# Ten extra products on TensorE between attention and the first tile of experts, and the early batches' sums moved ahead of b1's transpose

## The chip, the cores and the metric

The kernel runs on one core of a Trainium2 chip. The metric is the device time of one execution in microseconds (us). Engines: PE (TensorE), DVE (VectorE), ACT (ScalarE), POOL (GpSimd) and SP (SyncE, which here only issues DMAs).

## The reference

A gated cross-attention layer and a gated mixture of experts, over 8 batches of 112 tokens with 256 features:

```
x = x + tanh(g_xattn) * xattn(ctx, layernorm(x))      # 8 heads of 64, 375 context rows a batch, rotary keys
h = layernorm(x)
P = softmax(h @ Wg); top 2 of 8 experts, gates P_norm = P_topk / (sum P_topk + 1e-9)
y = sum over e of P_norm[e] * (gelu(h @ W1[e] + b1[e]) @ W2[e] + b2[e])   # W1: 256x1024, W2: 1024x256
x = x + tanh(g_ffn) * y
```

## The kernel before

The program has two blocks. `attention` works batch after batch and, beside its last heads, normalizes the rows for the experts and routes the first six batches (EARLY): top two experts, gates, and the slot in DRAM at which each token's row is kept for each of its two experts. The last two batches (LATE) finish attention only at the block's end.

`experts` is the second block, and the change lies in its PE part. Each engine has its own queue and goes through it in order; semaphores tie them together. What it does before the first tile:

- SP loads b1 as rows (`b1rows`, semaphore `small_loaded`), then b2 in eight copies (`b2x`), then expert 2's weights, then the rows of tiles 0 and 1 (`load_rows`, after all 16 scatters have landed), then stores `x_all` (after `b2_added` 4) and loads expert 3's weights.
- PE transposes b1rows into the bank `pm[0]` (L1545). Into the bank `pm[1]` it forms `sums`: the base (L1548), one product for each of the six early batches (L1551), and after `hits_done` 2 the late batches' (L1554) and the slots (L1556), which raises `slot_done`. It then transposes the gates `pnorm` (L1560, after `gated` and `b1t_done`), multiplies them by b2 in four products (L1568, after `pT_done`), and transposes the rows of tile 0 (`turn_rows`, L1578).
- DVE picks the late batches' two experts, forms their gates (to L143), waits for `slot_done`, makes the slots (`place`, L147 to L151), copies b1's transpose (`b1t`), works out the plan of the extra tiles (L1458 to L1476), the low half of W2 (L1479) and pT (L1482), and adds each b2 product to x_all (L1486). The third and fourth b2 product reuse a bank and wait for the first and second addition.
- POOL scatters the late batches' rows to their slots, two scatters a batch (L155), once the slots are there.
- ACT splits tile 0's transposed rows into high and low parts (`th`), DVE makes `tl`, and with it the first up product can run.

Then come 14 tiles of 256 rows. A tile has 48 up products (L1593 to L1595) and 48 down products (L1612 to L1614), in fp32r, three to each exact product; a bank `ph` takes up products, `py` down products. An f32 matmul of the program stands in the trace as two instructions. `ph[0]` is first written by the first up products.

Of the kernel before, what the change touches and what calls it, by code (L numbers as in the profile page):

```python
# [20 lines left out]
B, M, D = 8, 112, 256  # L21
# [3 lines left out]
E, FF = 8, 1024  # L25
# [10 lines left out]
FB = FF // P  # L36
# [1194 lines left out]
def experts(nc, w1, b1, w2, b2, out, rows_dram, acc_dram, x_all, rows1, rows2, router, ident, gates, w1s, w2s, w1n, w2n, wide, deep,  # L1231
            logit, w1_loaded, w2_loaded, w1h_done, w1l_done, w2h_done, w2l_done, filled):

    with ExitStack() as st:  # L1234
        def sb(name, shape, dt=F32):
            return st.enter_context(nc.sbuf_tensor(name, shape, dt))

        def ps(name):
            return st.enter_context(nc.psum_tensor(name, [P, 512], F32))

        def sem(name):
            return st.enter_context(nc.semaphore(name))
# [11 lines left out]
        b1rows = sb("b1rows", [E * FB, P])  # L1254
# [16 lines left out]
        ph = [ps(f"ph{n}") for n in range(3)]  # L1271
        pm = [ps("pm0"), ps("pm1")]

        small_loaded, b2_loaded = sem("esmall_loaded"), sem("b2_loaded")
        ptables_set, b2x_set, plan_done = sem("ptables_set"), sem("b2x_set"), sem("plan_done")
        ptr_done, pT_done, btr_done, b1t_done = (sem(n) for n in ("eptr_done", "pT_done", "btr_done", "b1t_done"))
# [264 lines left out]

        @block.tensor
        def _(pe):
            pe.wait_ge(small_loaded, 16)
            pe.transpose(pm[0][:, 0:E * FB], b1rows[:], ident[0:E * FB, 0:E * FB]).then_inc(btr_done, 1)  # L1545
            sums = pm[1][0:M, 0:3 * E].rearrange("q (b e) -> q b e", e=E)
            hit = router.hit
            pe.matmul(sums, router.ones[:], router.base[:].rearrange("q (a e) -> q a e", a=1).broadcast_to([M, 3, E]),  # L1548
                      start=True, stop=False)
            for b in range(B - 2):  # L1550
                pe.matmul(sums, router.ones[:], hit[:, b:b + 1].broadcast_to([M, 3, E]), start=False, stop=False)  # L1551
            pe.wait_ge(router.hits_done, 2)
            for b in range(B - 2, B):
                pe.matmul(sums[:, b - B + 3:3], router.ones[:], hit[:, b:b + 1].broadcast_to([M, B - b, E]),  # L1554
                          start=False, stop=False)
            pe.matmul(sums[:, 0:2], router.lower[:], hit[:, LATE], start=False, stop=True) \  # L1556
                .then_inc(router.slot_done, 1)
            pe.wait_ge(router.gated, 4)
            pe.wait_ge(b1t_done, 1)
            pe.transpose(pm[0][0:E * B, 0:M], router.pnorm[:].rearrange("q b e -> q (b e)"), ident[0:M, 0:M]) \  # L1560
                .then_inc(ptr_done, 1)
            pe.wait_ge(pT_done, 1)
            pe.wait_ge(b2_loaded, 16 * B)
            pe.wait_ge(plan_done, 2)
            for n in range(B // 2):
                if n >= 2:
                    pe.wait_ge(b2_added, n - 1)
                pe.matmul(pm[n % 2][0:M, :], pT[:], b2x[:, 2 * n:2 * n + 2].rearrange("q b d -> q (b d)"),  # L1568
                          start=True, stop=True).then_inc(b2_done, 1)

            def turn_rows(i):
                pe.wait_ge(xt_loaded[i % 3], 16 * (i // 3 + 1))
                if i:
                    pe.wait_ge(tl_done, i)
                for k in range(KD):
                    for n in range(2):
                        c = k * T + n * P
                        last = pe.transpose(pxt[:, c:c + P], xt[i % 3][:, n, k * P:(k + 1) * P], ident[:])  # L1578
                last.then_inc(tr_done, 1)

            def up(i, g):
                n = i * GRP + g
                if g == 0:
                    pe.wait_ge(w1l_done, KD * (i + 1))
                    pe.wait_ge(tl_done, i + 1)
                if n >= 3:
                    pe.wait_ge(gelu_done, n - 2)
                p = i % 2
                for u in range(2):
                    dst = ph[n % 3][:, u * T:(u + 1) * T]  # L1590
                    c = slice((2 * g + u) * P, (2 * g + u + 1) * P)
                    for k in range(KD):
                        pe.matmul(dst, w1h[p][:, k, c], th[:, p, k], start=k == 0, stop=False)  # L1593
                        pe.matmul(dst, w1h[p][:, k, c], tl[:, p, k], start=False, stop=False)  # L1594
                        last = pe.matmul(dst, w1l[p][:, k, c], th[:, p, k], start=False, stop=k == KD - 1)  # L1595
                last.then_inc(up_done, 1)

            def down(i, g):
                n = i * GRP + g
                if g == 0 and i:  # L1600
                    pe.wait_ge(y0_done, i)
                    pe.wait_ge(y1_done, i)
                if g % 2 == 0:
                    pe.wait_ge(w2l_done, 2 * i + g // 2 + 1)
                pe.wait_ge(hl_done, n + 1)
                p = i % 2
                for u in range(2):
                    f = 2 * g + u
                    for s in range(2):
                        c = slice(s * P, (s + 1) * P)  # L1610
                        dst = py[s][:, 0:D]
                        pe.matmul(dst, hh[:, n % 3, u, c], w2h[p][:, f], start=f == 0, stop=False)  # L1612
                        pe.matmul(dst, hh[:, n % 3, u, c], w2l[p][:, f], start=False, stop=False)  # L1613
                        last = pe.matmul(dst, hl[:, n % 3, u, c], w2h[p][:, f], start=False, stop=f == FB - 1)  # L1614
                last.then_inc(down_done, 1)

            turn_rows(0)
            for i in range(TILES):
                up(i, 0)
                if i:  # L1620
                    down(i - 1, 2)
                up(i, 1)
                if i:
                    down(i - 1, 3)
                up(i, 2)
                if i + 1 < TILES:
                    turn_rows(i + 1)
                down(i, 0)
                up(i, 3)
                down(i, 1)  # L1630
            down(TILES - 1, 2)
            down(TILES - 1, 3)
# [32 lines left out]
```

## Time and profile before

| | |
|---|---|
| time, 3 runs | 526.6 us median, 524.97 to 527.88 |
| the profiled execution | 523.4 us, span 521.7 us, mean granted PE clock 0.928 |
| PE busy | 446.3 us, 86% of the span |
| PE weight loads busy | 373.2 us, 72% |
| DVE, ACT, POOL busy | 289.4, 295.1, 195.4 us |

The span is from the first to the last instruction of the profiled execution. The granted clock is TensorE's, as a share of 2.4 GHz: 1.00 is that, 0.50 is 1.2 GHz. "Idle before" is the time an engine stood idle ahead of an instruction, with what ended it.

### The profile page before, as it was taken

The page shows a single profiled execution, that of the slowest core. Times are in us where ns is not written, and L with a number is a line of the kernel's source. Part 1 is how long each engine was busy: PE and PEld are TensorE (multiplying, and loading weights), DVE is VectorE, ACT ScalarE, POOL GpSimd, SP SyncE. Part 2 cuts the span into 40 slices and gives each one's busy share as a digit, 9 for nine tenths or more (in the row PEclk, how much of TensorE's full clock was granted, in tenths as well). Part 3 has the DMA queues.
Part 4 walks back from the last instruction along what each step waited for, and adds up shares of the span by engine and source line. Part 5 has one row for each costly group of instructions (what it writes and reads, how often), then busy time and mean ns, then how long its engine had stood idle before and what let it go on. Part 6 is the DMA issues. An engine that isn't in the chain of part 4 may idle for free. (4 is left out here: it accounts for less than half of the span.)

```text
span 521.7 us, 9510 instructions
## 1 busy us (share of the span) xinstructions
PE 446.3 (86%) x3237; PEld 373.2 (72%) x3237; DVE 289.4 (55%) x707; ACT 295.1 (57%) x652; POOL 195.4 (37%) x223
## 2 busy tenths in 40 slices
PE   2674699999989999899998764589999999999990
PEld 1453476766767677676776643279999999999990
DVE  3784324244451634435254823558888888888850
ACT  3534466765666666766767411056667667776730
POOL 4530163462825538164460165302222222333222
PEclk9976699999999999999999875569999999999997
DMA  7400010000000008999000021785777778775323
GB/s 190 117 29 1 1 31 0 9 24 2 29 1 24 5 0 252 226 215 319 12 2 1 1 71 44 233 254 175 212 204 212 219 223 232 224 206 132 44 29 90
DMA packets 41864, 56.04 MB, mean 107 GB/s; under 512 B 1745, under 2 KB 37153, under 8 KB 41808
## 3 DMA queue, kind: packets, MB, share of 16 engines
q1 hardware_dynamic: 36864, 49.80, 32.2%
q0 software_dynamic: 4960, 5.72, 7.1%
q8 instruction: 23, 0.38, 0.3%
q14 instruction: 17, 0.14, 0.1%
HBM read 40.37 MB, written 16.07 MB: 108 GB/s over the span
## 5 line engine op out<-in xcount | busy, mean ns | idle before, releaser
L1367 POOL DMA_INDIRECT acc_scratch<-yv,xt x28 | 49.2, 1757 | 130.6 <-DVE yv L1520 126.3
L1389 ACT ACTIVATE hf<-ph,b1t 128x256 f32<-128x256 f32 x112 | 47.0, 471 | 48.4 <-PE ph L1595 47.8
L871 DVE TENSOR_REDUCE negmax<-sc 112x1 f32<-112x487 f32 x64 | 42.2, 660 | 46.4 <-PE sc L1103 46.4
L691 ACT ACTIVATE prob<-sc,negmax 112x487 f32<-112x487 f32 x64 | 43.5, 680 | 12.6 <-DVE negmax L871 9.4
L1128 PEld LDWEIGHTS po<-probt,vals 125*64 125x64 f32 (+1 forms) x512 | 25.4, 139 | 23.5 <-issue 15.6
L699 ACT COPY probt<-pt 125x448 f32<-125x448 f32 x64 | 34.7, 542 | 11.1 <-PE pt L1111 10.9
L1103 PE MATMUL sc<-keys,queries 64*112 64x488 f32 x128 | 35.3, 629 | 6.1 <-ACT keys L640 3.4
L1502 DVE TENSOR_TENSOR hl<-hf,hh 128x512 fp32r<-128x512 f32 x56 | 38.8, 693 | 1.9
L1111 PEld LDWEIGHTS pt<-ident,prob 112*125 112x125 f32 x256 | 36.6, 191 | 4.2
L1111 PE MATMUL pt<-ident,prob 112*125 112x112 f32 x256 | 38.3, 274 | 0.0
L1500 DVE CAST hh<-hf 128x512 fp32r<-128x512 f32 x56 | 24.2, 433 | 23.7 <-ACT hf L1389 23.2
L379 POOL TENSOR_TENSOR krot<-krow,rope_t 125x512 f32<-125x512 f32 x21 | 27.0, 1285 | 22.1 <-ACT krow L618 22.0
L492 POOL TENSOR_TENSOR cl<-cf,ch 128x250 fp32r<-128x250 f32 x24 | 17.5, 728 | 45.3 <-ACT ch L612 45.3
L1593 PE MATMUL ph<-th,wide_h 128*128 128x256 f32 x112 | 32.6, 291 | 1.5 <-DVE tl L1491 1.5
L1128 PE MATMUL po<-probt,vals 125*64 125x112 f32 (+1 forms) x512 | 32.5, 270 | 1.2 <-ACT probt L699 1.2
L880 DVE TENSOR_TENSOR heads<-out_t,po 128x112 f32<-128x112 f32 x32 | 8.7, 271 | 43.4 <-ACT out_t L707 43.4
L1594 PE MATMUL ph<-tl,wide_h 128*128 128x256 f32 x112 | 32.5, 290 | 0.0
L1595 PE MATMUL ph<-th,wide_l 128*128 128x256 f32 x112 | 32.3, 288 | 0.0
L1612 PE MATMUL py<-deep_h,hh 128*128 128x256 f32 x112 | 32.0, 285 | 0.0
L1612 PE MATMUL py<-w2h_odd,hh 128*128 128x256 f32 x112 | 31.9, 285 | 0.0
L1593 PE MATMUL ph<-th,w1h_odd 128*128 128x256 f32 x112 | 31.6, 282 | 0.0
L1594 PE MATMUL ph<-tl,w1h_odd 128*128 128x256 f32 x112 | 31.6, 282 | 0.0
(273 smaller groups left out, 1372.1 us busy)
## 6 DMA issues: line engine op xcount, KB each, us to landing
w_next<-in_L_ffn_W SPq DMA_DIRECT2D x10, 1024.0 KB
rows_scratch<-blank SPq DMA_DIRECT2D x2, 4257.0 KB, 33.4
w_third<-in_L_ffn_W SPq DMA_DIRECT2D x8, 1024.0 KB
w1s<-in_L_ffn_W SPq DMA_DIRECT2D x5, 1024.0 KB
w2s<-in_L_ffn_W SPq DMA_DIRECT2D x5, 1024.0 KB, 8.7
xt<-rows_scratch SPq DMA_DIRECT2D x14, 258.0 KB, 2.8
ctx_t<-in_ctx SPq DMA_DIRECT2D x8, 375.0 KB
w1s<-in_L_xattn_Wkv SPq DMA_DIRECT2D x1, 1024.0 KB, 12.3
```

The costliest lines, as they stand in the source:

```text
L691: act.activation(prob[:, h % 2, 0:JA], sc[h % 2][0:M, 0:JA], ACT.Exp, bias=negmax[:, h % 2:h % 2 + 1], accum_out=total[:, p, h:h + 1]).the ...
L699: act.copy(probt[:, h // 2 % 2, :, h % 2, :], pt[h % 2][0:JR, 0:NT * M].rearrange("q (a r) -> q a r", a=NT)) \
L871: dve.tensor_reduce(negmax[:, h % 2:h % 2 + 1], sc[h % 2][0:M, 0:JA], AX, ALU.max, negate=True).then_inc(max_done.sem, 1)
L1103: pe.matmul(sc[u][0:M, 0:JP], queries[r, p, a], keys[r, p, a], start=True, stop=True, tile_position=(u * DH, 0)).then_inc(score_done.sem, 1)
L1111: last = pe.transpose(pt[h % 2][0:JR, j * M:(j + 1) * M], prob[:, h % 2, j * JR:(j + 1) * JR], ident[0:M, 0:M])
L1128: pe.matmul(po[r, 0:M], vals[0:rows, p, j, a * P + u * DH:a * P + (u + 1) * DH], probt[0:rows, a % 2, j, u], start=j == 0, stop=j == NT - ...
L1367: pool.indirect_dma_start(out=acc_dram, out_offset=bass.IndirectOffsetOnAxis(ap=xt[i % 3][:, n, D + 1:D + 2].bitcast(I32), axis=0), in_=yv ...
L1389: last = act.activation(hf[:, n % 3, u], ph[n % 3][:, u * T:(u + 1) * T], ACT.Gelu, bias=b1t[:, col])
L1502: dve.tensor_tensor(hl[:, n % 3], hf[:, n % 3], hh[:, n % 3].bitcast(F32), ALU.subtract) \
L1593: pe.matmul(dst, w1h[p][:, k, c], th[:, p, k], start=k == 0, stop=False)
L1594: pe.matmul(dst, w1h[p][:, k, c], tl[:, p, k], start=False, stop=False)
L1612: pe.matmul(dst, hh[:, n % 3, u, c], w2h[p][:, f], start=f == 0, stop=False)
```

## The change

PE gets a helper `idle(n)` that issues n products nobody reads: the identity's first 112 rows (112 x 128) as weights, 512 columns of `rows1` as data, f32, into `ph[0]`. It is called with 2 at five places: at the block's start, after b1's transpose, after the slots' product, after the transpose of the gates, and ahead of `turn_rows(0)`. The base product and the six early batches' products now stand ahead of the wait for b1's rows and of b1's transpose.

```
-            pe.wait_ge(small_loaded, 16)
-            pe.transpose(pm[0][:, 0:E * FB], b1rows[:], ident[0:E * FB, 0:E * FB]).then_inc(btr_done, 1)
+            def idle(n):
+
+                for _ in range(n):
+                    pe.matmul(ph[0][:], ident[0:M, :], rows1[:, 0:2, 0:D], start=True, stop=True)
+
+            idle(2)
             sums = pm[1][0:M, 0:3 * E].rearrange("q (b e) -> q b e", e=E)
             hit = router.hit
             pe.matmul(sums, router.ones[:], router.base[:].rearrange("q (a e) -> q a e", a=1).broadcast_to([M, 3, E]),
                       start=True, stop=False)
             for b in range(B - 2):
                 pe.matmul(sums, router.ones[:], hit[:, b:b + 1].broadcast_to([M, 3, E]), start=False, stop=False)
+            pe.wait_ge(small_loaded, 16)
+            pe.transpose(pm[0][:, 0:E * FB], b1rows[:], ident[0:E * FB, 0:E * FB]).then_inc(btr_done, 1)
+            idle(2)
             pe.wait_ge(router.hits_done, 2)
...
             pe.matmul(sums[:, 0:2], router.lower[:], hit[:, LATE], start=False, stop=True) \
                 .then_inc(router.slot_done, 1)
+            idle(2)
             pe.wait_ge(router.gated, 4)
             pe.wait_ge(b1t_done, 1)
             pe.transpose(pm[0][0:E * B, 0:M], router.pnorm[:].rearrange("q b e -> q (b e)"), ident[0:M, 0:M]) \
                 .then_inc(ptr_done, 1)
+            idle(2)
             pe.wait_ge(pT_done, 1)
...
+            idle(2)
             turn_rows(0)
```

## Rows read from the trace of the kernel before

**Rows 1.** The page: PE's busy share in 40 slices of the span, in tenths

```profile
PE   2674699999989999899998764589999999999990
```

**Rows 2.** Stretches of the span: length, busy us (x count) of each engine, PE clock, DMA

```profile
290.00:345.00 55.00, 32.46 (x164) 23.47 (x164) 25.17 (x107) 9.83 (x23) 21.11 (x43) 0.62 0.33 99
345.00:521.00 176.00, 164.68 (x1386) 164.47 (x1385) 135.35 (x191) 108.60 (x191) 49.19 (x28) 0.98 0.65 177
```

**Rows 3.** The chain that ended last, through the seam: start, us, what

```profile
320.29 2.29 DMA b1rows<-in_L_ffn_b
...
322.63 0.37 PE pm L1545
...
326.45 0.40 PE pm L1556 x2
...
327.70 0.17 DVE slots L151
...
332.46 0.20 DVE pT L1482
...
342.45 0.55 PE ph L1593
```

**Rows 4.** Timeline of PE through the seam: start, us, line, tiles, count, idle before

```profile
307.12 3.42 PE L1225 MATMUL po<-wof,heads 128*112 128x256 f32 x8 [1.00 <-DVE heads L880]
...
322.92 0.57 PE L1548 MATMUL pm<-base,ones 112*112 112x24 f32 x2
...
325.56 0.89 PE L1554 MATMUL pm<-hit,ones 112*112 112x16 f32 x4
...
328.14 0.37 PE L1560 MATMUL pm<-ident,pnorm 112*64 112x112 f32 x1 [1.31 <-DVE b1t L1456]
332.70 7.16 PE L1568 MATMUL pm<-b2x,pT 64*112 64x512 f32 x8 [4.19 <-DVE pT L1482]
339.79 1.11 PE L1578 MATMUL pxt<-ident,xt 128*128 128x128 f32 x4
```

**Rows 5.** Timeline of the other engines there, and the landing of xt's loads

```profile
322.69 0.24 DVE L126 TENSOR_TENSOR hit<-first,second 112x16 f32<-112x16 f32 x1
...
324.95 0.22 DVE L143 TENSOR_SCALAR rows<-red,gates 112x2 f32<-112x2 f32 x1
...
333.58 0.94 POOL L155 DMA_INDIRECT rows_scratch<-rows,slots  x1 [0.30 <-issue]
333.69 0.31 PEld L1568 LDWEIGHTS pm<-b2x,pT 64*112 64x112 f32 x1 [0.55 <-issue]
334.54 0.31 PEld L1568 LDWEIGHTS pm<-b2x,pT 64*112 64x112 f32 x1 [0.55 <-issue]
334.78 0.75 DVE L1486 SCALAR_TENSOR_TENSOR x_all<-pm,gates,x_all 112x512 f32<-112x512 f32 x1 [2.14 <-issue]
...
336.37 0.88 SPq L1298 DMA_DIRECT2D xt<-rows_scratch  x2
...
DMA to landing us min/median/max: 2.7/2.9/3.0
```

**Rows 6.** Stretches around the clock's changes, and the steady tiles; columns as above

```profile
294.00:296.40 2.40, 0.14 (x2) 0.00 (x0) 2.23 (x8) 1.03 (x4) 0.00 (x0) 1.00 0.00 0
307.10:310.00 2.90, 2.88 (x7) 2.18 (x8) 0.00 (x0) 0.00 (x0) 2.02 (x3) 0.50 0.26 80
310.50:313.40 2.90, 0.04 (x1) 0.00 (x0) 1.81 (x10) 0.00 (x0) 2.18 (x3) 1.00 0.28 85
313.50:342.40 28.90, 14.74 (x44) 8.91 (x44) 13.52 (x56) 2.88 (x5) 11.78 (x32) 0.50 0.43 136
332.70:339.70 7.00, 7.00 (x8) 2.18 (x8) 2.25 (x3) 0.00 (x0) 1.52 (x2) 0.50 0.48 145
342.45:347.60 5.15, 5.15 (x24) 5.15 (x25) 1.31 (x3) 2.20 (x4) 0.00 (x0) 0.50 0.98 292
360.00:500.00 140.00, 140.00 (x1190) 140.00 (x1190) 118.58 (x166) 94.91 (x166) 42.78 (x24) 1.00 0.67 181
```

**Rows 7.** The chain that ended last, where the clock changes: start, us, what

```profile
347.49 0.21 PE ph L1594
...
347.84 0.12 PE ph L1593
```

More of the change, by code:

```diff
@@ L1543, in _, with idle @@
         def _(pe):
-            pe.wait_ge(small_loaded, 16)
-            pe.transpose(pm[0][:, 0:E * FB], b1rows[:], ident[0:E * FB, 0:E * FB]).then_inc(btr_done, 1)
+            def idle(n):
+                for _ in range(n):
+                    pe.matmul(ph[0][:], ident[0:M, :], rows1[:, 0:2, 0:D], start=True, stop=True)
+            idle(2)
             sums = pm[1][0:M, 0:3 * E].rearrange("q (b e) -> q b e", e=E)
@@ L1551, in _ @@
                 pe.matmul(sums, router.ones[:], hit[:, b:b + 1].broadcast_to([M, 3, E]), start=False, stop=False)
+            pe.wait_ge(small_loaded, 16)
+            pe.transpose(pm[0][:, 0:E * FB], b1rows[:], ident[0:E * FB, 0:E * FB]).then_inc(btr_done, 1)
+            idle(2)
             pe.wait_ge(router.hits_done, 2)
@@ L1557, in _ @@
                 .then_inc(router.slot_done, 1)
+            idle(2)
             pe.wait_ge(router.gated, 4)
@@ L1561, in _ @@
                 .then_inc(ptr_done, 1)
+            idle(2)
             pe.wait_ge(pT_done, 1)
@@ L1615, in down @@
                 last.then_inc(down_done, 1)
+            idle(2)
             turn_rows(0)
```

## Prediction

> **What bounds the kernel now.** Start with the page's forty slices [rows 1]: PE is nearly full from the sixth slice on and again in the experts, with one trough around slices 23 to 26. The table by stretches says what the trough is [rows 2]: from 345 to 521 us PE is busy 164.7 of 176 us at 0.98 of full clock, but from 290 to 345 us it is busy 32.5 of 55 us at 0.62. So the experts are bound by TensorE's pace, and whatever moves the start of the first tile moves the end by as much: about 100 products in 11.8 us for a tile, with DVE at 118.6 of 140 us and ACT at 94.9 behind it (1190 products in that stretch, 100 to a tile) [rows 6].
>
> The chain of waits through the seam [rows 3] gives the path: b1's rows land at 322.58, PE transposes them, forms the base product and the six early batches' sums (to 325.56 [rows 4]), the late sums and slots (to 326.85), DVE turns these into slots (to 327.87) and into the plan, deep_l and pT (to 332.66), PE multiplies by b2 (to 339.86 [rows 4]), transposes the first rows, ACT and DVE split them, and the first up product starts at 342.45. Beside it runs a second path that the chain does not print: slots, four scatters on POOL (the last issued at 333.58, with 0.94 us), the row loads on SP at 336.37, landing in 2.7 us at the earliest, so at 339.1 [rows 5]. It ends only 0.7 us ahead of the transposes at 339.79 [rows 4]. Both paths hang on the slots.
>
> **The clock.** In the seam the granted clock is 0.50 (1.2 GHz) from 313.5 on, after PE had worked 0.04 us from 310.5 to 313.4, and it returns to 1.00 (2.4 GHz) only at 347.6, 5.15 us into the up products [rows 6]. These 24 products run at 0.21 us each, against 0.12 after it [rows 7]. At the high level they would take 24 x 0.12 = 2.8 us, so 2.3 us is what a high clock in the first tile is worth. The b2 products did not bring it back: PE busy 7.0 of 7.0 us, clock 0.50 to the end [rows 6].
>
> **What one idle product costs.** The trace has none. Its form is f32, 112 rows by 128 columns with 512 moving. The nearest is L1568, f32, 64 rows, 512 moving: two instructions for each product. Two loads of weights that follow each other begin 0.85 us apart (333.69 and 334.54) [rows 5], so an instruction takes that, 1.7 us a product and 3.4 us a pair at 1.2 GHz. The output projection L1225, 128 rows and 256 moving, has 8 instructions in 3.42 us, 0.43 each and half as many columns, so rows do not matter [rows 4]. Bounds: 3.6 us a pair with L1568's own mean (7.16 / 4 = 1.79) [rows 4], and half of 3.4, 1.7 us, at 2.4 GHz, as the fp32r products nearly halve. I take 3.4 low and 1.7 high. All five pairs are 8.5 to 18 us of TensorE time; the question is how much of it finds a hole.
>
> **Pair 1 and the sums ahead of b1.** PE can begin at 320.3, when SP issues b1's load [rows 3]. Today it waits until 322.6. The base and early sums take 325.56 - 322.92 = 2.64 us [rows 4]. Without the idle products the sums would be finished at 322.95, just as DVE gives the late hits (322.69 + 0.24 [rows 5]); the late part and its drain take 326.85 - 325.56 = 1.3 us, and DVE is busy with the gates until 325.2 [rows 5]. So moving the sums alone would start DVE's placing 1.7 us earlier (325.2 for 326.88). With pair 1 ahead at 1.2 GHz: 320.3 + 3.4 + 2.6 + 0.3 (b1's transpose, 322.63 to 322.92) = 326.6. That transpose, now later, is covered: DVE copies b1t only after placing, at 327.78, and ACT wants it for the first gelu.
>
> **Pair 2** stands before the late sums with nothing to cover it: the hits are ready at 322.9. 326.6 + 3.4 + 1.3 = 331.3, against 326.85: **slots 4.5 us later**. If pair 1 brings the clock up, every term after it halves: 323.7 + 1.4 + 0.2 + 1.7 + 0.7 = 327.7, **0.9 us later**. In no case are they earlier. Behind the slots wait DVE (place, b1t, plan, deep_l, pT: 332.65 - 326.85 = 5.8 us), POOL's scatters, and in SP's queue the row loads, the store of x_all and expert 3's weights. These come up to 4.5 us later, but expert 3 is the fourth tile, 35 us on.
>
> **Pairs 3 and 4** stand in holes: 1.3 us before pnorm's transpose (326.83 to 328.14) and 4.2 before the b2 products [rows 4]. Low clock: 3.4 + 0.3 + 3.4 = 7.1 us in a space of 6.0 (5.8, and 0.2 of drain ahead of the slots), so 1.1 over; with one of them at 2.4 GHz they fit.
>
> **b2 and pair 5.** At 1.2 GHz the b2 products take 7.1 us. At 2.4 they would take 3.4 alone, but the third and fourth each wait for a DVE addition of 0.75 us [rows 5]: about 3.9. Pair 5 comes directly behind, where PE now goes on within 0.1 us, so its cover is only the wait for the rows: after low b2 products none (3.4 us exposed), after fast ones all (1.7 us in a gap of about 2).
>
> **The sums.** (a) Slots 4.5 late, clock up by pair 4: b2 starts 337.2, ends 341.1, pair 5 342.8; the rows, 339.1 + 4.5 = 343.6, are last; 2.66 us from transposes to up [rows 4], less 0.4 for faster transposes: up at 345.9, +3.4, less 2.3 for the tile: **+1.1**. (b) Slots 0.9 late, but PE then has pairs 3 and 4 done by 331.2 and idles 2.4 us before pT and the clock is lost, as it was when PE did 0.14 us of work from 294 to 296.4 [rows 6]: b2 at 333.6, ends 340.7, pair 5 344.1, up at 346.7, +4.3, less 2.3: **+2.0**. Both are one forecast, that the pairs' exposed time outweighs the 2.3 us by a little; I take the upper, +2.0, since pair 1 starts at 0.50 in every case and one dip more is likelier than none. The profiled execution took 523.4 us about a span of 521.7, 3.2 below the median 526.6; shifting the median, **528.6 us**. The likeliest case's own range is 527 to 530.5.
>
> **Rivals.** Half a per cent is 2.6 us, about what a measurement here can tell from no change.
> *Clock up at once and kept* (the other side). All from pair 1's end runs at 2.4: slots +0.9, b2 333.6 to 337.5, pair 5 to 339.2, rows at 340.0, up at 342.3, tile -2.3: -2.5, 524.1 us; to -4 if pair 1 itself is partly fast. For it: after the projection, 2.88 of 2.90 us busy in f32, the clock was up [rows 6], and a pair is as dense. Against it: the 64-row b2 products, equally dense, left it low, and a hole of 2.4 us remains. It decides when the clock holds through that hole. The Trainium skill ("TensorE: Matmul & The Clock Gate", What's actually happening) says that activity releases the throttle and idling brings it back, which taken at its word would give this rival; the trace agrees for the projection and not for L1568's products.
> *Clock lost around pair 5.* As (b) with the 24 products still slow: +4.3, 530.9; or slots 4.5 late and b2 low: 337.2 + 7.1 + 3.4 + 2.7 = 350.4, +7.9 - 2.3 = +5.6, 532.2.
> *Low throughout*: b2 at 338.3, up at 351.5: +9.0, 535.6 us. For it: the low clock held for 34 us of the seam. Against: pairs 3 and 4 are almost 7 us of dense work with wider products than L1568.
> *All hidden*: the pairs fall wholly into idle time and the clock stays as it was, 0. Against: pair 5's place has no idle time.
>
> **Chances.** Forecast 0.41, lost around pair 5 0.26, low throughout 0.13, up and kept 0.15, hidden 0.05. Of "up and kept" 0.12 lies beyond 0.5% (it is -2.5 to -4); of the forecast 0.03 goes above. Faster 0.12, same 0.41 - 0.03 + 0.05 + 0.03 = 0.46, slower 0.26 + 0.13 + 0.03 = 0.42. The range leaves out most of "kept" and half of "low throughout": 525.0 to 533.0.
>
> **What would show it.** Idle pairs of about 3.4 us at clock 0.50 or 1.7 at 1.00; the slots' product at 327.7 to 331.3; the rows' loads moved by the same amount; clock 1.00 at the first up product, which comes at 345.5 to 347, with 0.12 us from product to product at once; the experts' 140 us stretch as before. I am wrong if the clock holds from pair 1 to the tile (up near 342), if it is low at the tile, or if an idle product's price is not 1.7 us.

## The result, and the profile after

The changed kernel takes 528.95 us (median of 22 runs, 525.21 to 531.6), the kernel before 525.55 (22 runs on the same chips). The ratio is 1.0058, with a 95% interval of 1.0039 to 1.0076: 3.0 us slower by the ratio (the two medians differ by 3.4), and the interval keeps clear of 1. The forecast was +2.0. The profiled execution took 528.1 us with a span of 526.3.

That span is 4.7 us longer than the 521.7 of before, but 2.8 of these lie ahead of the experts block, which begins (SP's load of b1) at 323.06 instead of 320.29. A second profile of the kernel before, among the experiments, begins it at 322.84, so these 2.8 us are scatter between executions. From the block's start to the end of the span the change takes 203.3 us (526.35 - 323.06), before 201.4 (521.67 - 320.29), and 201.0 in the second profile. All times "from the block's start" below are counted this way.

The chain that ended last of the changed kernel, through the seam, answers to [rows 3]: start, us, what.

```profile
323.11 3.65 PE ph L1547 x4
326.76 0.12 PE pm L1552 x2
326.88 1.18 PE pm L1555 x12
...
328.27 1.92 PE ph L1547 x4
330.18 0.30 PE pm L1561 x4
330.48 0.22 PE pm L1563 x2
...
330.73 0.19 DVE key L147
...
336.31 0.20 DVE pT L1482
...
336.55 6.98 PE pm L1577 x8
343.53 3.66 PE ph L1547 x4
347.19 0.45 PE pxt L1587 x4
...
349.18 0.36 PE ph L1602
```

L1547 is the idle product. Three pairs are on the chain: pair 1 whole (3.65 us), pair 2 whole (1.92, at the high clock), and pair 5 whole (3.66). Pairs 3 and 4 are not there: DVE's work from the slots to pT covers them. L1577, the b2 products, took 6.98 us, as before. DVE starts placing 7.67 us after the block's start, where it was 6.6 (326.88 - 320.29); the first up product comes at 26.1, where it was 22.2.

The table by stretches of the changed kernel answers to [rows 6]: length, busy us (x count) of PE, PE loads, DVE, ACT, POOL, then PE clock and DMA.

```profile
323.10:326.50 3.40, 3.39 (x4) 1.46 (x5) 2.88 (x17) 1.15 (x2) 2.85 (x23) 0.50 0.08 18
326.60:332.40 5.80, 5.80 (x31) 3.68 (x30) 2.62 (x17) 0.00 (x0) 0.00 (x0) 1.00 0.56 180
334.40:336.50 2.10, 0.00 (x0) 0.00 (x0) 1.99 (x7) 0.00 (x0) 1.80 (x2) 1.00 0.88 293
336.80:343.40 6.60, 6.60 (x8) 1.76 (x7) 2.25 (x3) 0.00 (x0) 1.26 (x2) 0.50 0.40 115
343.50:347.00 3.50, 3.50 (x5) 1.36 (x5) 0.75 (x1) 0.00 (x0) 0.00 (x0) 0.50 0.49 138
...
349.20:352.00 2.80, 2.80 (x24) 2.80 (x25) 0.26 (x1) 1.54 (x4) 0.00 (x0) 1.00 0.97 375
...
365.00:505.00 140.00, 140.00 (x1190) 140.00 (x1190) 118.00 (x165) 94.93 (x166) 42.78 (x24) 1.00 0.67 182
```

Pair 1 runs at 1.2 GHz and the clock is up right behind it. From pair 4's end PE has no work for 2.2 us, and the clock falls 0.3 us into the b2 products and is down for the rest of them and for pair 5. It is up again for the first tile, whose 24 products pass in 2.8 us instead of 5.15. The steady tiles are as before, 1190 products in 140 us. So in this execution the first up product is 4.0 us late (26.12 against 22.16), 2.3 come back in the first tile, and the block ends 1.9 us late; the last 0.2 us lie elsewhere.

### The profile page after: what moved, and what is told of

It is laid out like the page before. It is cut to its first block and busy times, and to the rows that moved or that the text cites. A ratio compares the mean times of both kernels' runs of the same rounds, so it can differ in the third digit from the quotient of the medians.

```text
span 526.3 us, 9550 instructions
## 1 busy us (share of the span) xinstructions
PE 454.8 (86%) x3257; PEld 374.2 (71%) x3257; DVE 289.3 (55%) x707; ACT 295.1 (56%) x652; POOL 195.3 (37%) x223
## 5 line engine op out<-in xcount | busy, mean ns | idle before, releaser
L1128 PEld LDWEIGHTS po<-probt,vals 125*64 125x64 f32 (+1 forms) x512 | 25.4, 139 | 23.5 <-issue 15.6
L1602 PE MATMUL ph<-th,wide_h 128*128 128x256 f32 x112 | 31.4, 281 | 1.5 <-DVE tl L1491 1.5
L1622 PE MATMUL py<-deep_l,hh 128*128 128x256 f32 x112 | 31.5, 281 | 0.0
L1623 PE MATMUL py<-deep_h,hl 128*128 128x256 f32 x112 | 31.5, 281 | 0.0
```

The costliest lines, as they stand in the source:

```text
L1128: pe.matmul(po[r, 0:M], vals[0:rows, p, j, a * P + u * DH:a * P + (u + 1) * DH], probt[0:rows, a % 2, j, u], start=j == 0, stop=j == NT - ...
```

## The experiments

Times are medians; each ratio is to runs of the kernel before on the same chip. no_pair2, w_later_34 and w_later_fill ran on another chip than the other experiments, so kernels are compared by their ratios. "Weights later" is an edit shown further down; every experiment has the sums moved as in the change.

| kernel | idle products at the five places | runs | time, us | ratio, 95% |
|---|---|---|---|---|
| the change | 2 2 2 2 2 | 22 | 528.95 | 1.0058, 1.0039 to 1.0076 |
| sums_only | 0 0 0 0 0 | 12 | 526.55 | 1.0003, 0.9984 to 1.0023 |
| early_pairs | 2 2 0 0 0 | 9 | 529.04 | 1.0068, 1.004 to 1.0096 |
| late_pairs | 0 0 2 2 2 | 12 | 525.33 | 0.9987, 0.9969 to 1.0005 |
| no_pair5 | 2 2 2 2 0 | 12 | 529.1 | 1.006, 1.004 to 1.008 |
| no_pair2 | 2 0 2 2 2 | 12 | 525.27 | 0.9979, 0.9959 to 0.9999 |
| rows64 | 2 2 2 2 2, of 64 rows | 4 | 535.86 | 1.018, 1.0151 to 1.0209 |
| w_later | 0 0 0 0 0, weights later | 9 | 523.84 | 0.9954, 0.9934 to 0.9974 |
| w_later_pairs | 0 0 2 2 2, weights later | 6 | 522.62 | 0.9927, 0.9908 to 0.9946 |
| w_later_34 | 0 0 2 2 0, weights later | 8 | 523.51 | 0.9949, 0.9926 to 0.9972 |
| w_later_fill | 0 0 2 2 1 and 2 behind the rows' transpose, weights later | 6 | 520.48 | 0.99, 0.9875 to 0.9925 |

**Which pairs cost.** Five kernels, edited as the table says, each from the change. The edit of no_pair2, for instance:

```
             pe.transpose(pm[0][:, 0:E * FB], b1rows[:], ident[0:E * FB, 0:E * FB]).then_inc(btr_done, 1)
-            idle(2)
             pe.wait_ge(router.hits_done, 2)
```

> All ten idle products out, the early sums still ahead of b1's transpose. Theory A (the pairs' exposed time is the loss, the moved sums are a gain of their own): DVE's placing starts 1.7 us earlier counted from the experts block's start, the clock stays low to the first tile, the time is 1.3 to 2.2 us below before. Theory B (the loss is not the pairs' but lies ahead of the seam: the changed kernel's experts block began at 323.07 where it began at 320.29 before): 1 to 3 us above before, as the rest of the kernel is as in the change. Theory C (the moved sums are worth nothing, something else is last): the same as before within 0.5 us.

Measured: 1.0003. A, B and C named three outcomes; the time is C's. B is out: the blocks of the experiments began at 322.0 to 323.5, whatever the edit (and at 320.8 in no_pair2's profile). The trace shows the first half of A and the reason of C. DVE starts placing 4.8 us after the block's start (328.24 - 323.45), 1.8 earlier than before, as A says, and the b2 products begin 1.8 earlier as well. But then something else is last, and the gain is lost behind them. Timeline of sums_only, the last scatter, SP's loads and the first rows' transpose:

```profile
323.45 0.58 SPq L1288 DMA_DIRECT2D b1rows<-in_L_ffn_b  x1
...
328.62 0.39 SPq L1305 DMA_DIRECT2D w_third<-in_L_ffn_W  x1
329.06 0.46 SPq L1308 DMA_DIRECT2D w_third<-in_L_ffn_W  x1
...
334.05 7.17 PE L1573 MATMUL pm<-b2x,pT 64*112 64x512 f32 x8 [4.18 <-DVE pT L1482]
...
334.94 0.94 POOL L155 DMA_INDIRECT rows_scratch<-rows,slots  x1 [0.30 <-issue]
...
339.92 0.88 SPq L1298 DMA_DIRECT2D xt<-rows_scratch  x2
...
342.63 1.11 PE L1583 MATMUL pxt<-ident,xt 128*128 128x128 f32 x4 [1.41 <-DMA xt<-rows_scratch]
```

POOL has issued the last scatter at 335.88, but SP, which waits for its landing, loads the rows only at 339.92, 4.0 us on. Before it was 1.9 us (334.52 to 336.37, [rows 5]). PE then waits 1.41 us for the rows. The rows' load is 16.5 us from the block's start, against 16.1 before: the slots came early and the rows did not.

> Only pairs 1 and 2, the sums moved. Theory A2: slots 1 to 4.5 us late and nothing back, since the clock is lost again before the first tile: +2.5 to +4 us over before. Theory A1: 0 to +1 us.

Measured: +0.68%, as A2. In the profiled execution placing began 11.3 us from the block's start, 4.7 late, and the clock stayed low from before the block to past the first up product. Stretch of early_pairs from pair 1 to the slots' product, columns as above:

```profile
322.10:333.30 11.20, 11.19 (x29) 6.74 (x29) 4.11 (x24) 1.15 (x2) 2.86 (x23) 0.50 0.48 163
```

Here two pairs of 112 rows and the sums, 11.2 us without a gap, were not followed by the high clock, where pair 1 alone was in the profile of the change. The code is the same up to there.

> Pairs 1 and 2 out, pairs 3, 4, 5 kept, the sums moved. Theory A2: slots 1.7 us earlier than before from the block's start; pairs 3 and 4 bring the clock up before b2, pair 5 is then partly hidden behind the rows; 2 to 4 us below before (about 522.5), with some runs above. Theory A1 (pair 5 is the loss): no better than before, 0 to +2 us.

Measured: -0.13%, with an interval that holds no change: A2's 2 to 4 us didn't come, and A1's 0 to +2 isn't excluded by this kernel alone. The rows' load was at 16.2 us from the block's start here too (338.33), the same wall as in sums_only. The b2 products took 3.92 us at the high clock, but PE then waited 2.2 us for the rows, and the first tile began at the low one.

> Only the pair ahead of the first rows' transpose out. Theory A1 (pair 5 alone is the loss, 3.66 us directly on the path): the time falls to about before, -0.3 us or less. Theory A2 (the pairs ahead of the slots are the main loss; pair 5 gives back in the first tile's clock about what it costs): it stays 2 to 3.5 us above before, and in some runs the first tile runs at the low clock.

Measured: +0.60% with pair 5 gone, +0.58% with it. A1 falls, A2 holds. Pair 5 is wholly on the chain of the change (3.66 us), and yet no net cost is seen; the 1.3 us that 3.66 less the tile's 2.3 leaves would lie within the intervals. In the profiled execution without it the first up product came at 26.1 us from the block's start and the clock was not up before 30.4. That profile is not the change's less pair 5: its placing began 10.7 us from the block's start, as the clock rose only at the end of pair 2. PE then idled 2.2 us ahead of b2, as in the change, and the b2 products took 6.99 us, again at the low clock.

> The changed kernel without pair 2 alone. Theory P2 (pair 2 has no cover at all and pair 1 only part of one): slots 2.7 us after before's when the clock stays low less pair 2's 3.4, so 0 to 1.2 us late (place at 6.6 to 7.8 from the block's start), the time within 1.5 us of before. Theory P1 (pair 1 at the block's start costs as much as pair 2): it stays 1.5 us or more above before.

Measured: -0.21% (0.9979) against +0.58% with pair 2: its absence is worth 0.8%, 4 us. P2 holds. The profiled execution took 522.15 us, one of three near 522; the other nine took 524.98 to 526.34. Timeline of PE in no_pair2, whose block begins at 320.79:

```profile
320.84 3.58 PE L1547 MATMUL ph<-rows,ident 112*128 112x512 f32 x4 [2.64 <-PEq L205]
...
326.27 0.35 PE L1562 MATMUL pm<-hit,lower 112*112 112x16 f32 x2
326.46 1.96 PE L1547 MATMUL ph<-rows,ident 112*128 112x512 f32 x4
...
332.47 5.70 PE L1576 MATMUL pm<-b2x,pT 64*112 64x512 f32 x8 [2.21 <-DVE pT L1482]
```

The slots' product starts 5.5 us from the block's start, earlier than before (326.30 - 320.29 = 6.0) although pair 1 is ahead of it: the moved sums run at the high clock. Placing begins at 5.9, earlier than P2's 6.6 to 7.8, which were for the low clock. Pair 1 has no cost that can be told: no_pair2 differs from late_pairs by pair 1 alone, 0.9979 against 0.9987. Pair 2, behind it, costs 4 us.

**What the clock answers to.** The same kernel with idle products of half the rows.

```
-                    pe.matmul(ph[0][:], ident[0:M, :], rows1[:, 0:2, 0:D], start=True, stop=True)
+                    pe.matmul(ph[0][:], ident[0:64, :], rows1[0:64, 0:2, 0:D], start=True, stop=True)
```

> The changed kernel with idle products of 64 rows instead of 112; nothing else differs, and the products' own time should not (L1225 and L1568 agreed on that). Theory R (the granted clock answers to how much of the array a product fills: the b2 products with 64 rows kept it at 0.50 for 7 us): the clock stays at 0.50 from the block's start to the first tile, all pairs take 3.4 us, b2 starts about 18 us after the block's start, the time is 7 to 9 us above before. Theory S (any dense stream of products brings it up, b2's was held back by its waits for DVE): as the changed kernel, +3.4 us.

Measured: +1.8%, 9.5 us, a little past R's 7 to 9. Stretches of rows64, columns as above:

```profile
323.40:342.40 19.00, 19.00 (x38) 9.04 (x39) 9.22 (x49) 1.15 (x2) 7.54 (x27) 0.50 0.41 135
342.40:352.00 9.60, 9.60 (x13) 3.38 (x11) 3.00 (x4) 0.00 (x0) 0.21 (x1) 0.50 0.31 92
352.00:359.50 7.50, 5.95 (x25) 4.75 (x24) 0.89 (x2) 2.93 (x5) 0.00 (x0) 0.50 0.99 320
```

PE is busy in every one of 28.6 us and the clock stays at 0.50 throughout. Nothing but the number of rows differs from the change. With 112 rows the clock rose behind pair 1 (the change, no_pair2), at the end of pair 2 (no_pair5) or, where only pairs 3 and 4 stood ahead of b2, within pair 4 (late_pairs); where it didn't (early_pairs), only pairs 1 and 2 were there. So the high clock did not follow one pair of 112 rows every time, and in rows64 it did not follow five pairs of 64 rows and the b2 products at all. S is out, on one profile and four runs; widths other than 64 and 112 were not tried. It is also the "low throughout" rival, made to happen: +9.0 had been worked out for it, +9.5 measured (0.018 of 525.9).

**Where the moved sums' gain went.** Expert 2's weights, 2 MB, requested behind the first rows instead of ahead of them:

```
-            load_expert(2)
             load_rows(0, slice(0, T))
             load_rows(1, slice(REGION, REGION + T))
+            load_expert(2)
```

> No idle products, the sums moved, and expert 2's weights requested behind the first two tiles' rows instead of ahead of them. Theory W (with the sums alone the slots came 1.8 us earlier but the last scatter's landing, 4.0 us after its issue ended where it was 1.8 before, waited behind the 2 MB of weights): the last scatter lands 1.8 us after its issue, the row loads go out 14.2 to 14.5 us after the block's start (16.5 with the sums alone), b2's products are last again, the first up product comes at 20.4 (before: 22.16), about 1.7 us below before. Theory V (the landing is the scatter's own time, whatever else moves): the row loads stay at 16.1 to 16.5 and the time at before's.

Measured: -0.46%, 0.5% less than sums_only; W holds. Timeline of w_later:

```profile
323.32 0.58 SPq L1288 DMA_DIRECT2D b1rows<-in_L_ffn_b  x1
...
333.92 7.16 PE L1573 MATMUL pm<-b2x,pT 64*112 64x512 f32 x8 [4.18 <-DVE pT L1482]
...
334.80 0.94 POOL L155 DMA_INDIRECT rows_scratch<-rows,slots  x1 [0.30 <-issue]
...
337.39 0.91 SPq L1298 DMA_DIRECT2D xt<-rows_scratch  x2
...
341.01 1.11 PE L1583 MATMUL pxt<-ident,xt 128*128 128x128 f32 x4
```

From the last scatter's issue to the rows' load it is 1.65 us, where sums_only had 4.0; the load goes out 14.1 us from the block's start, 2.4 earlier, and the transposes follow the b2 products with no wait.

The DMA packets in the traces show the wait itself. The weights' packets run from 7.0 to about 13.4 us after the block's start in sums_only. Its first scatter is issued at 6.6, and its packets begin at 11.2; in w_later, with the same issue, they begin at 8.1. In before the weights run from 7.0 to about 12.8, and the last scatter, issued at 13.3, comes behind them. Two stretches of sums_only, with the DMA share and GB/s in the last two columns:

```profile
331.00:337.00 6.00, 2.95 (x4) 1.12 (x5) 3.47 (x13) 0.00 (x0) 3.96 (x4) 0.50 1.03 368
338.00:339.90 1.90, 1.90 (x3) 0.57 (x2) 0.95 (x2) 0.00 (x0) 0.00 (x0) 0.50 0.03 8
```

> As w_later, with pairs 3, 4 and 5 (not 1 and 2). Theory W and A2 together: b2 starts at 10.8 with the clock up and ends near 14.8, pair 5 ends at 16.5, the rows land at 17.0, the first up product comes at 19.2 with the clock up: 3 to 5 us below before (521 to 523). Theory V: as late_pairs, 0.6 us below.

Measured: -0.73%, 522.6, in the range of W and A2. The b2 products took 3.92 us instead of 7, pair 5 ended within the wait for the rows, and the first up product came at 19.6 (w_later 20.35), with the clock low for part of the first tile (it fell at 20.1 and rose at 23.5 us).

> w_later_pairs without pair 5, to see what pair 5 does once the rows land early. Theory K (pair 5 keeps the clock for the first tile and is covered by the wait for the rows): without it 0.5 to 2 us slower than w_later_pairs (523 to 524.6). Theory L (pair 5 is only a cost wherever it stands): 1 us or more faster than w_later_pairs (521.6 or less).

Measured: 0.9949, 0.2% behind w_later_pairs, with overlapping intervals. The direction is K's, its size is not settled. In the profile the clock, up for the b2 products, was down again from 16.9 us and rose at 23.7, so that the first up product (19.9) ran at the low one.

> w_later_pairs with one product ahead of the first rows' transpose and a pair behind it, where PE waits 1.5 us for ACT and DVE to split the rows. Theory K: the clock holds more often up to the first up product, 0.5 to 1.5 us faster than w_later_pairs (521 to 522). Theory M (the pair behind the transposes delays the first up product by what it exceeds the hole, and the clock is lost or kept anyway): the same or up to 2 us slower than w_later_pairs.

Measured: -1.0%, 5.3 us below before and, by the ratios, 1.4 below w_later_pairs. That is K's direction, but the two intervals overlap. Against w_later, without idle products, it is 0.54%, 2.8 us, and the intervals are apart. The edit, beside the weights':

```
-            idle(2)
+            idle(1)
             turn_rows(0)
+            idle(2)
```

Stretches of w_later_fill, whose first up product is at 341.23:

```profile
322.00:331.20 9.20, 8.79 (x27) 5.89 (x28) 7.78 (x47) 1.15 (x2) 4.83 (x26) 0.50 0.10 26
331.40:341.20 9.80, 8.43 (x22) 2.79 (x20) 4.88 (x7) 1.41 (x2) 2.77 (x2) 1.00 0.49 137
341.30:344.00 2.70, 2.70 (x25) 2.70 (x25) 0.22 (x1) 1.45 (x4) 0.00 (x0) 1.00 0.90 278
```

The clock, once up, holds to the first tile, although PE still waits 1.4 us for the rows between the single product and the transposes. The first up product is 19.2 us from the block's start, 2.9 earlier than before, and the block ends after 196.5 us instead of 201.4.

**The kernel before once more.**

> The kernel before, for a second profile. If its first profile (block start at 320.29, 2.1 us below the median time) was a fast one ahead of the seam, the experts block starts at 322 to 323.5 here, as in the others, and the stretch from there to the end is again 201.4 us. If the changed kernel really starts the block later, it starts near 320.3 again.

Measured: one run of 525.6 us; the block begins at 322.84 and lasts 201.0 us. The changed kernel doesn't start it later.

## Why the prediction was right

The sign holds, the time lies inside the range, and in the profiled execution the mechanism came as forecast. That the median lies 0.35 us from the forecast is partly luck: the median of before had been taken 1 us high, and the loss is 3.0 us where 2.0 were forecast.

- **Price of a pair**: 3.4 low and 1.7 high forecast; 3.65 and 1.92 on the chain. That rows do not matter held for the price (rows64), but not for the clock.
- **Pairs 1 and 2 delay the slots by 0.9 or 4.5 us**: 1.1 in the profiled execution of the change (7.67 against 6.6); 4.7 in early_pairs' and 4.1 in no_pair5's, whose code is the same up to the slots. The late slots of case (a) exist, then. The rest of (a), the clock kept for b2 behind pair 4, is in none of these profiles: no_pair5's lost it in the 2.2 us ahead of b2.
- **Case (b)**: in the profiled execution it came step by step. PE's idle time ahead of b2: 2.4 us forecast, 2.2 seen, and the clock lost there. The b2 products: 7.1 against 6.98. Pair 5: 3.4 against 3.66, exposed. The first up product: +4.3 against +4.0. The tile: -2.3, as seen. In all +2.0 against +1.9.
- **Pairs 3 and 4** were forecast to fit at the high clock, and neither is on the chain.
- **The whole**: +2.0 forecast, +3.0 measured. The profiled execution alone gives +1.9, so others must have cost more. 18 of the 22 runs lie between 528.07 and 531.6 and 4 between 525.21 and 526.22; which of the worked-out cases each one is, its time doesn't say. A likely part of the rest is executions with the clock still low at pair 2, as in two other profiles: slots 4.1 to 4.7 us late, and in no_pair5's the clock low again for b2. With pair 5 that is the rival worked out at 532.2, not the forecast. How often it comes in the changed kernel was not measured, and where the third microsecond lies stays open.
- **Within half a per cent or slower**: the chances gave 0.46 and 0.42. +0.58% is slower, but the interval, 0.39 to 0.76%, holds the boundary.
- **The step that failed**: "moving the sums alone would start DVE's placing 1.7 us earlier" is right (1.8), but the path of scatters and row loads was taken to move with the slots. It does when they are late (17.1 us from the block's start in the change, 20.6 in early_pairs, 16.1 before), but hardly when they are early: with expert 2's weights under way the load goes out at 16.5 in sums_only, 16.2 in late_pairs and 15.7 in no_pair2. This was outside the sum, because the change never got its slots early; sums_only shows it at its full size, 1.8 us gained and 0 kept.
- **Pair 5** was priced as 3.4 us exposed after slow b2 products, with 2.3 given back by the tile's clock, a net cost of about 1. Taking it out changed the time by 0.02%, with intervals that leave room for 1 us either way. It is pair 2 that turned a change of nothing into a loss.
- **The clock.** Two findings decide between the rivals: "up at once and kept" failed at the 2.2 us without work ahead of b2, after which the clock was down, and "low throughout" came only with the narrower products of rows64. The Trainium skill ("TensorE: Matmul & The Clock Gate", What's actually happening) has activity release the throttle. The changed kernel's trace agrees, with the clock up behind pair 1. In rows64, PE busy for 28.6 us at 0.50, and in early_pairs, 11.2 us, the traces don't, so "busy" in the profile's sense isn't enough.

## What to carry to other kernels

Filler for an engine's clock is worth its place only where the engine waits for something: count for each filler what is queued behind it. Here the pair with a ready consumer behind it (pair 2, ahead of the slots) cost 4 us. Filler in true waits, spread up to the dense work, brought 2.8 of the 5.3 us of w_later_fill; the other 2.4 came from the moved sums and weights without any filler (w_later). And when a chain is made to start earlier, look at the DMA traffic that it will now meet: the transfer that used to be over by then can take the gain back, and moving one request on the queue can free it.

## What the runs showed of the hardware

- f32 products of 64 rows and 512 moving columns, without a gap for 28.6 us together with the small ones, never raised the granted clock from 0.50 (rows64). A pair of 112 rows was followed by 1.00 in the changed kernel and in no_pair2; in early_pairs two such pairs, PE busy for 11.2 us, were not.
- An f32 product of 112 rows took as long as one of 64: 3.65 to 3.78 us a pair of 112 at 0.50 (the change, early_pairs), 3.62 to 3.78 a pair of 64 (rows64).
- From the end of the last scatter's issue (112 rows) to the rows' load that waits for it, it was 1.65 us with no weights under way (w_later), and 4.0 us with 2 MB of weights requested some 6 us ahead of it on another queue (sums_only). It was 1.85 us in the kernel before, where the weights had been requested 8 us ahead.
